# A decoder block on one core: the attention output weight turned and multiplied by the router's weight inside the attention loop instead of ahead of it

## What is computed

```python
x = layernorm(x + mixer(x))                     # W_in, W_gate, W_out, A, Bm, C, D
x = layernorm(x + cross_attention(x, ctx))      # Wq, Wk, Wv, Wo and their biases
x = layernorm(x + experts(x))                   # router Wr, br, then W_up, W_down

# cross attention, last line
return out @ Wo + bo
# experts, first lines
logits = xf @ Wr + br
Sm = softmax(logits)
G_t, idx_t = top_k(Sm.T, n_tok // E)
```

## Time and profile before

| | us |
|---|---|
| median of 3 runs | 296.9 (296.69 to 297.55) |
| the profiled execution | 296.91 |
| its span, first to last instruction | 295.1 |
| TensorE busy (matmul) | 247.5 |
| VectorE busy | 195.1 |
| ScalarE busy | 155.5 |
| GpSimd busy | 137.9 |

### The profile page before, as it was taken

How to read it: one execution, slowest core, us unless ns; L and a number is a source line. 1 busy time by engine, 2 the same in 40 slices (tenths; PEclk the granted TensorE clock), 3 DMA queues, 4 the chain that set the end, 5 groups by cost and what they waited for, 6 DMA issues and landing times.

```text
span 295.1 us, 5155 instructions
## 1 busy us (share of the span) xinstructions
PE 247.5 (84%) x1685; PEld 202.0 (68%) x1685; DVE 195.1 (66%) x615; ACT 155.5 (53%) x323; POOL 137.9 (47%) x205
## 2 busy tenths in 40 slices
PE   8999998989998999999998111257999999999990
PEld 4756556757565677989997111226999999999880
DVE  0744466245895857796999788772565966776495
ACT  3654522343449755546512367702747888874354
POOL 6812973342534430155577889227784043443000
PEclk9999999799999999999999855555899999999996
DMA  6961004003609292746910069903347665522655
GB/s 185 297 125 38 1 11 91 8 0 72 143 9 208 65 211 44 149 120 157 301 27 1 1 233 372 292 17 106 109 87 213 161 116 78 126 26 30 166 213 213
DMA packets 33676, 35.60 MB, mean 121 GB/s; under 512 B 10610, under 2 KB 25970, under 8 KB 33394
## 3 DMA queue, kind: packets, MB, share of 16 engines
q1 hardware_dynamic: 30130, 30.90, 38.1%
q0 software_dynamic: 2784, 4.00, 8.2%
q10 hardware_dynamic: 736, 0.38, 0.4%
HBM read 18.16 MB, written 8.19 MB: 89 GB/s over the span
## 4 chain that ended last, share of the span: by engine, by line
PE 57%; DVE 21%; ACT 9%; issue 6%; DMA 3%; POOL 3%; DVEq 0%; POOLq 0%; ACTq 0%; SPq 0%
PE bank L1233 12%; PE bank L1479 8%; PE bank L1702 6%; PE bank L1322 5%; PE bank L1430 4%; DVE junk L2088 3%; PE bank L1398 2%; PE bank L1413 2%; DVE NMF L1921 2%; PE bank L1466 2%; ACT bank L1150 2%; PE bank L1243 1%; DMA summed_rows<-OUT,idx 1%; DVE bn L1909 1%; PE bank L1658 1%
## 5 line engine op out<-in xcount | busy, mean ns | idle before, releaser
L892 POOL DMA_INDIRECT summed_rows<-OUT,idx x14 | 21.8, 1555 | 34.0 <-DVE OUT L2206 31.7
L819 POOL TENSOR_SCALAR var_eps<-mean_var 128x1 f32<-128x1 f32 x32 | 7.2, 224 | 61.3 <-DVE mean_var L1914 61.2
L1479 PEld LDWEIGHTS bank<-VB,PT 128*128 128x128 f32 x256 | 32.4, 191 | 1.9 <-DVE ATT L2003 0.2
L1479 PE MATMUL bank<-VB,PT 128*128 128x34 f32 x256 | 31.3, 270 | 0.0
L1233 PE MATMUL bank<-FTH,WUH 128*128 128x256 f32 x94 | 27.8, 295 | 0.1
L1233 PE MATMUL bank<-FTL,WUH 128*128 128x256 f32 x94 | 27.0, 287 | 0.0
L1233 PE MATMUL bank<-FTH,WUL 128*128 128x256 f32 x94 | 27.0, 287 | 0.0
L1150 ACT ACTIVATE bank<-bank,b_up_c 128x256 f32<-128x256 f32 (+1 forms) x48 | 19.5, 446 | 13.7 <-PE bank L1233 13.7
L1921 DVE TENSOR_REDUCE NMF<-bank 128x8 f32<-128x512 f32 x32 | 21.6, 680 | 6.5 <-PE bank L1442 6.3
L1702 PE MATMUL bank<-WDH,MH 128*128 128x256 f32 x80 | 23.2, 290 | 1.3 <-DVE ML L2220 1.3
L1003 ACT ACTIVATE PT<-bank 128x512 f32<-128x512 f32 x32 | 18.7, 597 | 10.0 <-PE bank L1466 9.9
(11 more groups left out here) (359 smaller groups left out, 735.2 us busy)
## 6 DMA issues: line engine op xcount, KB each, us to landing
WDR<-in_L_ffn_W_down SPq DMA_DIRECT2D x8, 640.0 KB
QS<-QH SPq DMA_DIRECT2D x32, 128.0 KB, 3.1
WUR<-in_L_ffn_W_up SPq DMA_DIRECT2D x4, 682.0 KB, 4.9
routed_rows<-X SPq DMA_DIRECT2D x2, 1056.0 KB, 11.1
X<-in_x SPq DMA_DIRECT2D x4, 512.0 KB, 5.0
QS<-QL SPq DMA_DIRECT2D x16, 128.0 KB, 2.9
summed_rows<-X SPq DMA_DIRECT2D x2, 1024.0 KB, 6.4
Y<-summed_rows SPq DMA_DIRECT2D x8, 256.0 KB, 5.5
```

The costliest lines, as they stand in the source:

```text
L892: pool.indirect_dma_start(summed, bass.IndirectOffsetOnAxis(ap=idx[:, 2 * e + h:2 * e + h + 1].bitcast(U32), axis=0), OUT[:, (2 * e + h) % ...
L1479: last = pe.matmul(o[:, j * 34:(j + 1) * 34], PT[m % 2][:, j, s * P:(s + 1) * P], VB[:, m // 2, j].rearrange("p h d -> p (h d)"), start=Tr ...
```

## The change

The turning of the output weight moves from unit -3 to unit 5, its product with the router's weight from unit -2 to unit 7. In those units both stand near the end of the unit on TensorE and ScalarE, and the subtraction WOL at the end of the unit on VectorE. Both products now use bank 0. `wo_s` and `wot_s` get memory of their own, and SP's wait goes. The bias part is no longer a product of 32 rows by one column: two products in unit 2, ahead of the first logits and in the same bank, make the eight numbers on all 128 rows (the bias broadcast as weight); ScalarE copies them, and VectorE adds them where it copied the turned logits before.

```diff
-    TURN_UNIT = -3
-    THROUGH_UNIT = -2
+    TURN_UNIT = 5
+    THROUGH_UNIT = 7
...
-        bo_through = place("bo_through", [P, 1], F32)
+        bo_through = place("bo_through", [P, E], F32)
...
+        wo_s = place("wo_s", [P, KC, D], F32)
+        wot_s = place("wot_s", [P, KC, D], F32)
...
-        wo_s = staged("wo_s", [P, KC, D])
-        wot_s = staged("wot_s", [P, KC, D])
...
+            if g == TURN_UNIT:
+                product("wot", 0)
+            if g == THROUGH_UNIT:
+                product("wrw", 0)
             if live(g, "att"):
...
                     sp.wait_ge(w_lo, 3)
-                    wait_moved(sp, "wrw")
...
                     wait_filled(act, ("lg", n))
                     if n == 0:
-                        wait_moved(act, "bow")
+                        act.activation(bo_through[:], bank_of(("lg", n))[:, P:P + E], ACT.Copy).then_inc(bo_out, 1)
                     else:
                         wait_filled(act, ("lgt", n - 1))
-                    act.activation(LGT[:], bank_of(("lg", n))[:, 0:P], ACT.Identity, bias=bo_through[:, 0:1])\
-                        .then_inc(sem_moved(("lg", n)), 1)
+                    act.activation(LGT[:], bank_of(("lg", n))[:, 0:P], ACT.Copy).then_inc(sem_moved(("lg", n)), 1)
+                if g == TURN_UNIT:
+                    wait_filled(act, "wot")
+                    act.activation(wot_s[:].rearrange("p c n -> p (c n)"), bank_of("wot")[:], ACT.Copy).then_inc(sem_moved("wot"), 1)
+                if g == THROUGH_UNIT:
+                    wait_filled(act, "wrw")
+                    act.activation(WO[0][:, :, D:RW], bank_of("wrw")[:, 0:KC * E].rearrange("p (c e) -> p c e", c=KC),
+                                   ACT.Copy).then_inc(through_hi, 1)
...
-                o = turn("bow")
-                for c in range(KC):
-                    for s in range(TPB):
-                        last = pe.matmul(o[32 * s:32 * s + 32, 0:1], wr_s[:, c, :], bo_c[:, c:c + 1],
-                                         start=(c == 0), stop=(c == KC - 1))
-                last.then_inc(sem_filled("bow"), 1)
...
                 o = turn(("lg", n))
+                if n == 0:
+                    for c in range(KC):
+                        pe.matmul(o[:, P:P + E], bo_c[:, c:c + 1].to_broadcast([P, P]), wr_s[:, c, 0:E],
+                                  start=(c == 0), stop=(c == KC - 1))
...
-                dve.tensor_copy(lgt[:, TPB * n:TPB * n + TPB, :], got).then_inc(sem_moved(("lgt", n)), 1)
+                dve.wait_ge(bo_out, 1)
+                dve.tensor_tensor(lgt[:, TPB * n:TPB * n + TPB, :], got,
+                                  bo_through[:].unsqueeze(1).to_broadcast([P, TPB, E]), ALU.add)\
+                    .then_inc(sem_moved(("lgt", n)), 1)
...
                 for part in TABLES_AT.get(g, ()):
                     masks(part)
+                if g == THROUGH_UNIT:
+                    through_low()
```

More of the change, by code:

```diff
@@ L410, in decoder_block @@
                 product("wrm", 0)
[L411 to L415, removed]
             for n in (2, 3):
@@ L550, in decoder_block @@
         ath_made = sem("ath_made")
-        biased_made, through_hi, lgt_added = sem("biased_made"), sem("through_hi"), sem("lgt_added")
+        biased_made, through_hi, lgt_added, bo_out = sem("biased_made"), sem("through_hi"), sem("lgt_added"), sem("bo_out")
         lm_made, ex_made, s2_made, routed_made = [
@@ L1047, in _ @@
                     normalise(1, g - 1 - LAG["z1"])
[L1048 to L1056, removed]
                 for q in GATE_UNITS.get(g, ()):
@@ L1554, in _ @@
                     router_sums()
[L1555 to L1558, removed]
                 for n in (2, 3):
@@ L1581, in _ @@
                     logits_transposed(block_of(g - TURN_LATER, "q"))
+                if g == TURN_UNIT:
+                    weight_turned()
+                if g == THROUGH_UNIT:
+                    router_through()
                 if live(g, "att"):
@@ L2012, in _ @@
                     centred()
-                if g == THROUGH_UNIT:
-                    through_low()
                 for n in (2, 3):
```

## The result

The changed kernel has a median of 292.39 us (four runs, 291.97 to 292.75) beside 296.79 for the kernel before: ratio 0.985 (95% interval 0.982 to 0.988), 4.4 us faster. The direction of the forecast was right; its 294.2 was 1.8 us too slow and the range began 0.4 us too high, at 292.8. The profiled execution took 291.97 us. Some executions of these kernels take 8 us or more longer at a lower granted clock; they are left out of every comparison, and the profiles of e4 and e8, which fell into such ones, with them.

A forecast was written before the change was run, and what follows sets the result against it. It took the lead-in's chain through TensorE, held up by a 1.75 us wait and then a falling granted clock, as the bound. Sum: 296.91 - 4.65 + 0.52 + 0 + 1.42 = 294.2 us; range 292.8 to 296.4.

The forecast's parts named there:

- bias part: Unit 2: two broadcast-bias products, four records ahead of the first logits, count in full on TensorE's chain; +0.52 us.
- lead-in: Ahead of the attention loop: without the moved work, block 0's queries start near 56.75 instead of 61.41; 4.65 us earlier.
- turning in unit 5: Four transposes, 0.44 us of TensorE, push back z1(11), but its VectorE reader is held anyway; taken as 0.
- hold in unit 8: Block 2's transposes wait for WOL to free bank 0, so its queries start at 93.85 instead of 92.43; +1.42 us.
- rest of the loop: From block 2's queries on, each step is fed by the one before, so nothing takes the delay back; 0.
- last release: Lead-in: ScalarE's gate copies and copies of the transposes end at 56.7, releasing block 0's queries at about 56.75.
- Rival 2: Unit 8: the hold costs nothing because the stretch behind it has slack; 292.8 us, chance 0.08.
- Rival 1: Granted clock falls once behind a new wait, before block 0's queries or in unit 8; costs 1.58, 295.8 us, chance 0.20.
- rival 3: Behind unit 8's wait the clock stays at 1.2 GHz through the following units; slower, 298 us or more, chance 0.07.

The follow-up runs named there:

- e4: Changed kernel with the product, WOH and WOL in unit 9 instead of unit 7; ratio 0.984 (0.981 to 0.987) to the kernel before.
- e8: Changed kernel once more, unaltered, beside the kernel before; ratio 0.985 (0.983 to 0.988), 4.4 us faster.
- e2: Kernel before with eight idle TensorE products filling its 1.75 us wait in the lead-in; ratio 0.991 (0.988 to 0.994), 2.7 us faster.
- e3: Changed kernel with ScalarE's copy WOH in unit 7 moved ahead of the table load and both exponentials; ratio 0.987 (0.983 to 0.991) to the kernel before.
- e7: Changed kernel with product, WOH and WOL in unit 9, plus idle TensorE products late in the search and ahead of the first expert; median 289.07 us, ratio 0.975.
- e12: Changed kernel with two idle ScalarE copies ahead of WOH in unit 7, lengthening the hold of bank 0; one execution, 294.41 us.
- e1: Kernel before with only the bias part of the change; ratio 1.0015 (0.999 to 1.004).
- e11: Kernel before once more, unaltered, for a second profile; no time of its own is stated.
- e5: Kernel before with idle TensorE products in the last steps of the search and ahead of the first expert; median 293.66 us, ratio 0.989 (0.987 to 0.991).

## Why the prediction was too small

The working of 4.94 us between the first two profiles (296.91 and 291.97), each step as the lead that it adds or costs:

| step | predicted | measured |
|---|---|---|
| start of the count | - | -0.09 |
| lead-in | +4.65 | +4.96 |
| bias part | -0.52 | -0.35 |
| turning in unit 5 | 0 | 0 |
| hold in unit 8 | -1.42 | -1.23 |
| rest of the loop | 0 | +0.14 |
| search | 0 | +0.35 |
| gather of the first expert's tokens | 0 | +0.11 |
| experts to TensorE's end | 0 | +1.45 |
| behind that, and outside the span | 0 | -0.40 |
| sum | +2.71 | +4.94 |

**Right.** The cause of the gain: TensorE's wait of 1.75 us, the transposes, the small matmuls and the clock's fall left the lead-in, and e2 shows the link between the wait and the fall by itself. The last release: the queries of block 0 do come behind ScalarE's copies. Unit 5: z1(11) lost 0.44 us of lead, its reader on VectorE none (4.61 us at 80.50, as for z1(8) at 66.38, counted from the centring product). Unit 8: a hold of bank 0 through WOH and WOL, with the transposes at 87.31, where 91.85 less the lead gives 87.3. Rival 2 (slack behind the hold) is out, by e3, e7 and e12. Rival 1 and rival 3 did not come about, but e12 shows rival 1's mechanism one microsecond of waiting further on.

**Where it failed.** The mechanism held and the sum was too small in two ways: three of its terms were mis-sized, and everything behind the loop was put at nothing without a reason.

**Wrong, in size.** The lead-in (4.65, measured 4.96), the bias part (0.52, measured 0.35) and the hold (1.42, measured 1.23) erred the same way, 0.31 + 0.17 + 0.19 = 0.67 us; 0.09 of it is the later start of the count, which the table's first row takes back. Each was priced by the listed length of a record. Queued back to back, the next instruction starts earlier: the two gate copies and the next copy are 1.14 us apart (54.27 to 55.41), not 1.38; the transposes of block 2 take 0.82 to the next start (87.31 to 88.13), not 1.04; the four records of the bias part, listed with 0.51, take 0.43 (65.37 to 65.80), and 0.08 of that did not reach the chain, here and in e1 (0.35 and 0.36); why is open.

**Wrong, left out.** The sum ended with the loop. Behind it came 0.35 us in the search, which e1 gives to the bias part, and the experts, whose length differs by up to 1.45 us between executions for a reason that is not in the change. With the leads at the first expert the change itself is worth 3.8 to 4.0 us (154.91 against 150.93 to 151.10), which is some 293 us, at the lower edge of the range; the 4.4 of the timed runs, 3.6 to 5.3 by the two intervals, includes that, and what they show beyond it is no more than the experts' spread. A range for this kernel should have been widened by the experts' spread, which one profile of the kernel before could not show.

**Open.** Why one instruction of the search starts 0.25 us late in some kernels; what sets the moments at which the clock falls and returns (in the lead-in the wait ends 4.5 us behind the centring product in all four profiles, and the fall comes at 6.7 in the first and at 5.7 to 5.8 in e11, e1 and e5), so that a wait's length need not be all that counts; and whether the clock always falls in the lead-in of the kernel before: two of its timed runs took 294.60 and 294.69 us at a mean granted clock of 0.926, where the others of the comparisons have 0.906 to 0.922, and no profile shows such a run.

## To carry to other kernels

Before sizing a move, look at the granted clock around the wait that it removes and around the one that it creates: here the fall behind a wait of 1.75 us cost nearly as much as the wait, the new wait of 1.57 kept the clock, and one of 2.59 lost it. Price queued work by the distance between starts, not by the listed length of a record, and give every stage behind the change a term, if only a spread. If a stage starts with TensorE at half clock, expect its length to differ between executions; compare kernels stage by stage from a common event, and keep a spread for that stage.

## What the runs showed of the hardware

- The granted clock returned 3.0, 5.6 and 5.9 us behind the same product of the same program in three executions, and the second expert began 12.9, 14.0 and 14.0 us behind that product: 1.1 us of a 290 us kernel.
- Idle products ahead of the experts brought 3.2 us (e5), a gain as large as most of the change's, with work whose result nobody reads.
- An edit in the loop (e1) took 0.33 us off the search that follows it, at one VectorE instruction that no longer started late.
